# Layer 1 of a graph-network kernel: destination matrices in a ring of ten, relation coefficients three batches ahead, node tiles finished later

## The reference

```python
h = jnp.maximum(_layernorm(x, axis=-1), 0.0)
hsrc = h[src]
coef = w_comp[etype]                      # 32 relations -> 8 bases
for b in range(8):
    msg = msg + hsrc @ weight[b] * coef[:, b][:, None]
msg = msg * norm                          # one weight per edge
node_repr = segment_sum(msg, dst)
x = x + relu(node_repr + bias_param)
```

## Time and profile before

| | us |
|---|---|
| median of 3 runs | 4969.57 |
| the three runs | 4946.70, 4969.57, 4996.18 |
| span of the profiled execution | 6157.9 |
| mean granted PE clock in it | 0.844 |
| PE busy, all matmuls | 4502.8 (73%) |
| POOL busy | 3237.6 (53%) |
| DVE busy | 2553.7 (41%) |
| ACT busy | 1022.9 (17%) |

### The profile page before, as it was taken

The page is one execution under the profiler, slowest core; times in us unless marked ns, Lnnn a source line. Parts: engine busy times, 40 slices in busy tenths (PEclk is TensorE's granted clock), DMA queues, the critical chain, the costliest instruction groups (busy, mean ns, idle before and its releaser), DMA issues.

```text
span 6157.9 us, 72323 instructions
## 1 busy us (share of the span) xinstructions
PE 4502.8 (73%) x25760; PEld 2814.8 (46%) x25760; DVE 2553.7 (41%) x8838; ACT 1022.9 (17%) x2922; POOL 3237.6 (53%) x3390
## 2 busy tenths in 40 slices
PE   3778477888775445446555788988888898888888
PEld 2556355566554334344444343434443444444344
DVE  6778444445443445555567422222222222222222
ACT  4656311111111000001222200000000000000001
POOL 3232365566555555555553365565656556565655
PEclk8888688899887666667767999989999999999999
DMA  5222222122222222222221555555555555555554
GB/s 136 77 83 79 77 56 52 51 58 59 55 55 57 67 70 75 68 68 69 65 71 42 160 173 159 171 158 164 172 167 164 166 178 166 161 174 161 165 170 135
DMA packets 455501, 686.46 MB, mean 111 GB/s; under 512 B 91793, under 2 KB 237879, under 8 KB 455120
## 3 DMA queue, kind: packets, MB, share of 16 engines
q1 hardware_dynamic: 341188, 454.71, 23.5%
q0 software_dynamic: 107584, 223.83, 14.0%
q10 hardware_dynamic: 6364, 3.20, 0.2%
HBM read 599.50 MB, written 82.31 MB: 111 GB/s over the span
## 4 chain that ended last, share of the span: by engine, by line
PE 42%; another core or an unknown queue 24%; DVE 18%; issue 11%; ACT 3%; DMA 1%; ACTq 0%; SPq 0%; DVEq 0%; POOL 0%; POOLq 0%
PE ps L2007 27%; PE ps L1751 5%; DVE E L2458 4%; DVE B L2538 2%; PE pt L2102 2%; DVE arena L2580 1%; PE ps L1828 1%; PE ps L2093 1%; PE pt L2038 1%; PE ps L2022 1%; DVE O L3023 1%; PE pt L1719 1%; ACT E L1561 1%; DVE scores L3019 1%
## 5 line engine op out<-in xcount | busy, mean ns | idle before, releaser
L2007 PE MATMUL ps<-arena,E 128*128 128x512 fp8e4 (+1 forms) x4900 | 1147.0, 385 | 93.6 <-issue 84.8
L2007 PE MATMUL ps<-arena,A 128*128 128x512 fp8e4 (+1 forms) x4900 | 1142.1, 385 | 62.4 <-issue 60.1
L1052 POOL DMA_INDIRECT arena<-table,src_i x810 | 776.9, 959 | 685.7 <-DMA table<-E 255.0
L1017 POOL DMA_INDIRECT E<-gat_table,src_i x782 | 759.3, 971 | 634.6 <-DVE arena L2580 367.7
L1052 POOL DMA_INDIRECT arena<-x_spill,src_i x810 | 775.3, 957 | 579.0 <-issue 225.8
L1002 POOL DMA_INDIRECT arena<-table,src_i x782 | 742.8, 950 | 583.5 <-issue 217.1
L1751 PE MATMUL ps<-E,arena 128*128 128x352 f32 (+22 forms) x2932 | 783.6, 421 | 241.1 <-DVE E L2458 155.4
L2007 PEld LDWEIGHTS ps<-arena,E 128*128 128x128 f16 x4900 | 471.4, 100 | 648.6 <-issue 193.9
L2007 PEld LDWEIGHTS ps<-arena,A 128*128 128x128 f16 x4900 | 472.9, 100 | 608.9 <-issue 154.8
L1751 PEld LDWEIGHTS ps<-E,arena 128*128 128x128 f32 x2932 | 515.4, 211 | 441.4 <-issue 195.5
L2909 DVE SCALAR_TENSOR_TENSOR C<-ps,sc_b,scores 128x128 f32<-128x128 f32 x490 | 138.9, 345 | 1295.1 <-PE ps L2022 769.3
(11 more groups left out here) (350 smaller groups left out, 4557.6 us busy)
## 6 DMA issues: line engine op xcount, KB each, us to landing
arena<-adj SPq DMA_DIRECT2D x180, 1024.0 KB
arena<-adj SPq DMA_DIRECT2D x90, 1088.0 KB
adj<-E SPq DMA_DIRECT2D x39, 784.0 KB
arena<-table,src_i POOLq DMA_INDIRECT x1592
O<-dst_rows SPq DMA_DIRECT2D x112, 224.0 KB
arena<-adj SPq DMA_DIRECT2D x20, 768.0 KB
x_spill<-A SPq DMA_DIRECT2D x55, 256.0 KB
arena<-x_spill,src_i POOLq DMA_INDIRECT x810
```

The costliest lines, as they stand in the source:

```text
L1017: pool.indirect_dma_start(out=att_rows[:, b % 3 * AB + at, :], out_offset=None, in_=gat_table, in_offset=bass.IndirectOffsetOnAxis(ap=src_ ...
L1052: pool.indirect_dma_start(out=y_rows[:, g % ERING, k, :], out_offset=None, in_=(table, x_spill)[half], in_offset=bass.IndirectOffsetOnAxis ...
L2007: mm = pe.matmul(chunk_banks[n % 2][:, 0:len(some) * P], y[:, i, h * D:(h + 1) * D], adj_ring[:, piece % ADJ_RING, 0:len(some), at:at + P] ...
```

## The change

`m_ring` has ten slots for six. `raw` has two slots, one in each bank of `pt[0]`, and `made_c` moves out of PSUM into SBUF (`arena`). PE computes the coefficients of three batches before its first tile, and after that those of batch c + 3 at tile 4 of batch c; DVE takes those of batch c + 1 at tile 5, behind a wait for its own `m_made`. ACT makes the one-hots four batches ahead, still in two slots. Mixes come 6 tiles after a node tile's last edge tile for 4, outs 20 for 8, and all that is counted from `second_at` moves with them.

```diff
-MS = 6
+MS = 10
+COEFS, HOT_AHEAD, TO_MIX, TO_OUT = 3, 4, 6, 20
-        m_ring = E[:, 2 * CB * P:2 * CB * P + MS * WD * BASES]...
+        m_ring = E[:, 4 * P:4 * P + MS * WD * BASES]...
+        made_c = arena[:, RING * D + 4 * P:RING * D + 4 * P + 2 * CB * BASES]...
-            for k, late in (("mix", 4), ("out", 8)):
+            for k, late in (("mix", TO_MIX), ("out", TO_OUT)):
# ACT
-                one_hot(0)
-                one_hot(1)
+                for c in range(HOT_AHEAD):
+                    one_hot(c)
-                    if c + 2 < BATCHES:
-                        one_hot(c + 2)
+                    if c + HOT_AHEAD < BATCHES:
+                        one_hot(c + HOT_AHEAD)
# PE
                     pe.wait_ge(sem("type_hot"), 2 * c + 2)
-                    if c:
-                        pe.wait_ge(sem("coef_made"), c)
+                    if c >= 2:
+                        pe.wait_ge(sem("coef_made"), c - 1)
                     for h in range(2):
-                        mm = pe.matmul(raw[:, h * STACK * BASES:(h + 1) * STACK * BASES], type_hot[:, c % 2, h, :], w_mix,
+                        at = c % 2 * 512 + h * STACK * BASES
+                        mm = pe.matmul(raw[:, at:at + STACK * BASES], type_hot[:, c % 2, h, :], w_mix,
-                coefficients(0)
+                for c in range(COEFS):
+                    coefficients(c)
-                    if k % CB == 2 and k // CB + 1 < BATCHES:
-                        coefficients(k // CB + 1)
+                    if k % CB == 4 and k // CB + COEFS < BATCHES:
+                        coefficients(k // CB + COEFS)
# DVE
-                raw, made_c = pt[0][:, 0:CB * BASES], pt[0][:, 512:512 + 2 * CB * BASES]
+                raw = [pt[0][:, at:at + CB * BASES].rearrange("p (k b) -> p k b", b=BASES) for at in (0, 512)]
-                    if at == 4 and c + 1 < BATCHES:
+                    if at == 5 and c + 1 < BATCHES:
+                        if c:
+                            dve.wait_ge(sem("m_made"), c * CB)
                         coefficients(c + 1)
```

More of the change, by code:

```diff
@@ L220, in build @@
         type_rows = E[:, 0:2 * 2 * P].bitcast(I32).rearrange("p (s k e) -> p s k e", s=2, k=2)
-        m_ring = E[:, 2 * CB * P:2 * CB * P + MS * WD * BASES].rearrange("p (s d b) -> p s d b", s=MS, b=BASES)
-        out_tmp = E[:, 2 * CB * P + MS * WD * BASES:2 * CB * P + MS * WD * BASES + P]
+        m_ring = E[:, 4 * P:4 * P + MS * WD * BASES].rearrange("p (s d b) -> p s d b", s=MS, b=BASES)
+        out_tmp = E[:, 4 * P + MS * WD * BASES:4 * P + MS * WD * BASES + P]
+        made_c = arena[:, RING * D + 4 * P:RING * D + 4 * P + 2 * CB * BASES].rearrange("p (s k b) -> p s k b", s=2, b=BASES)
         junk = E[:, 5120:5120 + ET]
@@ L327, in build @@
         for i in range(NT):
-            for k, late in (("mix", 4), ("out", 8)):
+            for k, late in (("mix", TO_MIX), ("out", TO_OUT)):
                 after_tile[k].setdefault(min(last_tile[2 * i + 1] + late, TILES), []).append(i)
-        second_at = [min(last_tile[2 * (r * T7 + T7 - 1) + 1] + 8, TILES) for r in range(PTN)]
+        second_at = [min(last_tile[2 * (r * T7 + T7 - 1) + 1] + TO_OUT, TILES) for r in range(PTN)]
         GAT_IN = PTN - 1
@@ L629, in relations @@
                     for r in range(GAT_IN):
-                        if second_at[r] // CB + 5 + 11 == c:
+                        if second_at[r] // CB + 5 + 11 + HOT_AHEAD - 2 == c:
                             gat_group(r)
-                    if c == 2:
+                    if c == HOT_AHEAD + 2:
                         sp.wait_ge(sem("flags_made"), 1)
@@ L651, in relations @@
                 for r in range(GAT_IN):
-                    if second_at[r] // CB + 5 + 11 >= BATCHES:
+                    if second_at[r] // CB + 5 + 11 + HOT_AHEAD - 2 >= BATCHES:
                         gat_group(r)
@@ L2423, in relations @@
             def relations():
-                raw, made_c = pt[0][:, 0:CB * BASES], pt[0][:, 512:512 + 2 * CB * BASES]
-                made_c = made_c.rearrange("p (s k b) -> p s k b", s=2, b=BASES)
+                raw = [pt[0][:, at:at + CB * BASES].rearrange("p (k b) -> p k b", b=BASES) for at in (0, 512)]
                 def coefficients(c):
@@ L2429, in coefficients @@
                     dve.wait_ge(sem("coef_raw"), c + 1)
-                    dve.tensor_tensor(made_c[:, c % 2, 0:n, :], raw.rearrange("p (k b) -> p k b", b=BASES)[:, 0:n, :],
+                    dve.tensor_tensor(made_c[:, c % 2, 0:n, :], raw[c % 2][:, 0:n, :],
                                       bc(weight_e[:, c * CB:c * CB + n], BASES), MUL).then_inc(sem("coef_made"), 1)
```

## The result

| | us |
|---|---|
| kernel before, median (4946.70 to 4996.18, 4 runs) | 4967.89 |
| changed kernel, median (5020.02 to 5071.36, 4 runs) | 5025.71 |
| ratio, 95% interval | 1.0126 [1.0087, 1.0165] |
| forecast, range | 4995, 4890 to 5080 |

What follows compares the result with a forecast made beforehand. The prediction took POOL's gathers to bound layer 1 in the runs, with PE just behind. From 4970 us, coupling 0, start 0, end 0 to 3 and port +25 gave 4995 us, range 4890 to 5080.

Steps and rivals of the forecast that it cites:

- What bounds layer 1: Layer 1: POOL's gathers, one every 1.25 us, 782 of them 978 us, bind it in the unprofiled runs.
- the whole sum of 4989: All four layers: the least time of each, 510 + 1020 + 1069 + 2390 us, set against the runs' median of 4969.57.
- stands just behind: Layer 1: PE needs 9.1 to 9.6 us a batch where POOL needs 10.0.
- Coupling: Layer 1, ring of ten and coefficients three ahead: DVE freed from PE's coefficients of the same batch, worth 0 in the runs.
- Mixes, outs, start, new wait: Layer 1: later mixes and outs, three batches' coefficients first, DVE's wait on its own m: 0 to +3 us.
- The port: Layer 1: m now reads two SBUF tensors, so gathers starting inside an m wait for it; +25 us, upper end 127.
- the slower rival: Layer 1: every gather starting inside an m instruction is held up; price 52 to 127 us, time 5022 to 5097, chance 0.30.
- the discount: Layer 1: the 52 us for held-up gathers was halved to +25 us, as POOL might not lead PE by enough.
- gathers in step: Layer 1: a gather that has waited then keeps time with the m instructions, so the next waits only 0.07 us.
- random phases: Layer 1: gathers start anywhere inside an m and wait 0.33 us on average, 384 of them, 127 us as upper end.
- The faster rival: Layer 1: PE's pauses also occur in the runs and its restarts cost 70 to 90 us; time 4880 to 4900, chance 0.26.
- The signs: Profile after: L2430 idle under 50 us, L1002 gathers' mean above 946 ns if m holds them up, POOL's wait for PE near 0.

Runs made afterwards that it cites:

- second profile: The kernel before, unchanged, profiled again with the experiments: measured 4932.68 us, span 4930.6 us.
- the first experiment: The kernel before with only `made_c` moved to SBUF: 5008.39 us against 4963.24, ratio 1.0084.

## Why the prediction was right or wrong

**What bounds layer 1** was right: POOL's gathers, 1.25 us each, and the stalls of the first trace not there in the runs. The second profile of the kernel before has 978.6 us where the sum had 978, and the profile with half of the gathers shows how much they cost. That the whole sum of 4989 came so near the median was in part luck, since its other terms were off and cancelled: the second profile puts layer 1's first gather at 568.4 us where I had DVE's 510 for layer 0, layer 2 takes 1125 us (1574.7 to about 2700) where I had 1069, and PE is busy for 2191.49 us in layer 3 where I had 2390, a figure from the disturbed execution (granted clock 1.00 against 0.94 in the earlier trace rows). The row after that window, for the second profile (busy us of PE, PEld, DVE, ACT, POOL, granted clock):

```profile
2700.00:4930.00 2230.00, 2191.49 (x13639) 1091.01 (x13636) 664.34 (x3379) 214.93 (x630) 1553.66 (x1620) 1.00 0.65 202
```

**PE "stands just behind", 9.1 to 9.6 us a batch**: wrong in size. With POOL relieved, layer 1's gathers span 803.2 us, 8.2 a batch. The 9.1 took every tile as full width, but only 343 of the 782 m instructions are 128x512. The 9.6 took PE's 943.95 us at a granted clock of 0.84; with half of the gathers PE is busy for 800.62 us of this layer, at a granted clock of 0.98 (582 to 1412 us).

**Coupling, 0**: right. DVE's idle time moved from the coefficients to m and nothing was gained; the versions with `made_c` in PSUM are at 0.9991 and 1.0000.

**Mixes, outs, start, new wait, 0 to 3**: right as far as one can measure; the version with one-hots two ahead and the one with three both have 978 us of gathers.

**The port, +25: the term that was mis-sized.** Mechanism, place and condition were as the slower rival said, and the price was 58 us in the runs and 67.4 us of gathers, inside its 52 to 127. The failed step is the discount: I had 52 us for gathers in step with runs of m, and halved it, because POOL might not lead PE and because "m instructions in pairs, paced by PE, meet gathers of the same pace". POOL leads by 175 us (978.6 against 803.2), so nothing absorbs the wait; and with DVE at PE's pace the gathers got longer, not shorter: 41.8 us in the old order, 67.4 to 82.1 in the new one. The number of hits was right: 384 gathers were to start inside an m, and 383 do in the changed kernel. The wait of each was 0.18 us (67.4 by 383) and 0.11 in the first experiment, between the 0.07 of gathers in step and the 0.33 of random phases. 52 without the discount would have been 5022, the near end of the slower case. The Trainium skill (SBUF — State Buffer, "Who interferes with whom") gives the condition as two SBUF inputs against a GpSimd instruction that reads SBUF; the trace agrees, 1020.4 us of gathers with two and 978.2 with one, whichever of the two it is.

**The faster rival** fell with the pauses: PE's wait for DVE is 0.3 us in the second profile before. What I expected of a profile after (layer 1 at 1150 to 1220 us) was tied to them as well; it is 1074 (601 to 1675). **The signs** named for the lock came as written: L2433 idle for 0.0 us, gathers at a mean of 1034 ns, POOL waiting for PE for 4.9 us. The last says little, since it was 3.7 before.

## What to carry to other kernels

Before loosening a hand-off, find out whether the engine that waits there is the one that binds: DVE's 318 us of waits for coefficients were worth nothing, because POOL's gathers set the pace. When an operand is moved from PSUM to SBUF to free a bank, count the SBUF tensors of the instruction that reads it and look at what POOL does meanwhile: here one 128-column table made 782 gathers 42 to 82 us longer in all, and in the old order putting the other operand into PSUM took it all back. When a trace's span is far above the medians, ask for a second one before its waits are used: PE's 155.4 us of waits for DVE were 0.3 us in the second.

## What was not expected of the hardware

A run of eight narrow DVE instructions (128x208, 2.85 us) held a gather from 618.52 until it was over: 2.59 us for one that takes 0.95. That gather did not get its turn between two of them. It is not the rule for such runs: the one at 615.76 did (1.08 us), and so did the one of the earlier trace rows, at 2523.34, between two instructions of 128x896. The second of those starts while the gather runs:

```profile
2523.95 1.09 DVE L2639 TENSOR_TENSOR C<-C,rows 128x896 f32<-128x896 f32 x1
```

What decides between the two cases is open.

DVE's own rows hardly show that it holds POOL up: m takes 478.4 us in all with one SBUF tensor and 483.1 us with two in the old order, while the gathers take 978.6 and 1020.4 us. Nor does a start inside an m cost anything by itself: in the second profile of the kernel before 383 gathers start inside one too, with one tensor in PSUM, and their mean stays at 948 ns.
